# Cross attention with scores from rounded parts, larger table units, and a batch's first keys, x and queries made among the output products of the batch before

## The reference

```python
# 2 x 1024 queries, 16 heads of 128; the kernel takes them as B = 4 parts of 512 rows
q = rmsnorm((hidden_states @ Wq).reshape(B, Sq, H, D), gq)
k = rmsnorm((encoder_hidden_states @ Wk).reshape(B, Skv, H, D), gk)
v = (encoder_hidden_states @ Wv).reshape(B, Skv, H, D)
scores = jnp.einsum('bqhd,bkhd->bhqk', q, k) * scale
attn = jax.nn.softmax(scores, axis=-1)
out = jnp.einsum('bhqk,bkhd->bqhd', attn, v).reshape(B, Sq, H * D) @ Wo

# sixth block: three weight matrices of 1376 x 512, each entry one of 16 table entries
w = lut[idx]
```

## Time and profile before

| | |
|---|---|
| median of 3 runs | 2866.39 us (2860.24 to 2870.24) |
| the profiled execution | 2869.41 us, span 2867.7 us |
| granted TensorE clock, mean | 0.956 |
| busy share of the span | PE 91%, DVE 71%, ACT 41%, POOL 23% |

### The profile page before, as it was taken

One profiled execution on the slowest core, in us unless ns is written; L12 is line 12 of the kernel. 1 busy time (PEld: TensorE's weight loads), 2 busy tenths in 40 slices (PEclk: granted clock), 3 DMA queues, 4 the chain that ended last, 5 costly groups with the idle time before them and its releaser, 6 DMA issues. The chain is left out here.

```text
span 2867.7 us, 29360 instructions
## 1 busy us (share of the span) xinstructions
PE 2611.8 (91%) x9682; PEld 1648.7 (57%) x9682; DVE 2025.8 (71%) x4017; ACT 1171.1 (41%) x2107; POOL 653.0 (23%) x569
## 2 busy tenths in 40 slices
PE   6998898899699788899899999999999998999998
PEld 2343433434278544666666665666566664588886
DVE  4889899899966377788857887688858886232322
ACT  4453543635333112555535554455535554021111
POOL 2445454456301355111101110111111110000000
PEclk8999999999899899999999999999999998999999
DMA  4112111112301211333333222322322214200000
GB/s 146 52 45 81 53 66 59 53 37 81 125 30 50 76 34 70 131 103 103 121 89 121 74 74 83 109 85 74 92 85 100 85 56 159 72 1 30 30 15 15
DMA packets 90785, 212.46 MB, mean 74 GB/s; under 512 B 9990, under 2 KB 34822, under 8 KB 86540
## 3 DMA queue, kind: packets, MB, share of 16 engines
q1 hardware_dynamic: 81324, 178.26, 19.2%
q0 software_dynamic: 5472, 21.01, 1.9%
q10 hardware_dynamic: 3840, 11.34, 1.1%
HBM read 164.11 MB, written 46.47 MB: 73 GB/s over the span
## 5 line engine op out<-in xcount | busy, mean ns | idle before, releaser
L2153 POOL TENSOR_TENSOR h<-du,Bb 128x1024 f32<-128x1024 f32 x128 | 312.1, 2440 | 239.4 <-DVE h L1698 235.9
L1693 DVE TENSOR_TENSOR_SCAN h<-bank,h 128x512 f32<-128x512 f32 x256 | 299.9, 1207 | 32.4 <-ACT bank L1300 24.8
L1300 ACT ACTIVATE bank<-dt,A 128x512 f32<-128x512 f32 x256 | 175.6, 690 | 322.4 <-DVE h L1693 321.5
L1482 ACT ACTIVATE p<-bank,sm,rq 128x512 f32<-128x512 f32 x256 | 199.1, 778 | 245.1 <-DVE sm L2068 245.1
L2231 POOL TENSOR_TENSOR rq<-rq,mhalf 128x4 f32<-128x4 f32 x64 | 69.4, 1084 | 795.1 <-DVE rq L2022 795.1
L263 POOL TENSOR_SCALAR rstd<-mv 128x1 f32<-128x1 f32 x96 | 29.7, 310 | 949.9 <-DVE mv L257 949.9
L656 PE MATMUL bank<-pT,v 128*128 128x512 f32 x512 | 239.2, 611 | 2.7 <-ACT pT L1191 2.7
L656 PE MATMUL bank<-kr,q 128*128 128x512 f32 x512 | 233.6, 599 | 0.0
L870 PE MATMUL bank<-h,ident 128*128 128x512 f32 x256 | 147.3, 658 | 55.0 <-DVE h L1698 54.4
L995 PE MATMUL bank<-x_hi,wxq_s 128*128 128x512 f32 x512 | 188.9, 450 | 6.5 <-DVE x_lo L2043 6.5
L1978 DVE COPY_PREDICATED val<-msk,val 128x258 f32<-128x258 int32 x448 | 173.9, 451 | 28.2 <-DVE val L1978 0.5
(11 more groups left out here) (239 smaller groups left out, 5555.7 us busy)
## 6 DMA issues: line engine op xcount, KB each, us to landing
wxq_s<-wq_dram SPq DMA_DIRECT2D x48, 512.0 KB, 4.4
Bb<-bc_dram SPq DMA_DIRECT2D x32, 512.0 KB, 3.7
Cb<-bc_dram SPq DMA_DIRECT2D x32, 512.0 KB, 3.6
x_dram<-xo POOLq DMA_DIRECT2D x16, 1024.0 KB, 4.7
xc<-x_dram SPq DMA_DIRECT2D x16, 1024.0 KB, 5.3
woh<-in_Wo SPq DMA_DIRECT2D x64, 256.0 KB, 2.7
wxv_s<-wkv_dram SPq DMA_DIRECT2D x12, 1024.0 KB, 5.8
wxk_s<-wkv_dram SPq DMA_DIRECT2D x12, 1024.0 KB, 7.7
```

The source lines that it names most:

```text
L1300: act.activation(bank[2 + n][:, :], dt[:, c % 2, et, :], ACT.Exp, scale=A[:, et, 2 * w + n:2 * w + n + 1]).then_inc(dA_ready, 1)
L1482: act.activation(p4[:, t, :], bank[4 + t][:, :], ACT.Exp, bias=sm4[:, 4 + t:5 + t], scale=rq[:, hh % 2, 1, t:t + 1], accum_out=sm4[:, 8 + ...
L1693: dve.tensor_tensor_scan(h[:, s, n, :], bank[2 + n][:, :], h[:, s, n, :], 0.0, ALU.mult, ALU.add).then_inc(scanned, 1)
L2153: pool.tensor_tensor(h[:, G % HR, :, :], du[:, et:et + 1, :].to_broadcast([P, 2, S]), Bb[:, w % 2, :, :], ALU.mult).then_inc(dBu_ready, 1)
```

## The change

1. **Scores from rounded parts.** `scores` becomes 12 matmuls over `q_hi`, `q_lo`, `k_hi`, `k_lo` (fp32r). ScalarE's copy of q is now the rounded part; after `kr` it makes `k_hi`. VectorE makes `q_lo` (`q_rest`, from PSUM) and `k_lo` (`k_rest`). `scores` waits for both, and the bank that held q is free only after `q_rest`. q, k and their parts have one buffer each.
2. **Table units of 128 x 516**, 32 of them. A unit is cut into `masks`, `first_pair`, `second_pair`, `third_pair` and `fourth_pair`, in which each predicated copy follows its two entries. Batches 0 to 3 take 6, 8, 7 and 8 units in their heads (`LUTS`), and one unit each is made among the output products of batches 0, 1 and 2 (`LATE`).
3. **Order on VectorE.** `key_scale` comes before the scaling of the weights, `query_mean` before most of the look-up, and in batch 0 the rests of `wxq` at the end of the head. The key norms write one mean for each tile, and GpSimd raises four small tiles instead of one.
4. **Order between batches.** Keys 0 and 1 of the next batch are made before `turn_weights(15)`, keys 2 and 3 around `weighted(15)`, x after it, the queries of head 0 after output product 8, its keys' transposes and squares after product 10, and the values of group 0 behind product 15. Every step on the other engines moves with them; SP loads the next batch's x at head 12 instead of after its last weight.
5. `TILES4` is one list over all batches; the buffers of the output product lie over `p4` and `pT`, so that ScalarE writes the first `w_hi3` only after `weighted(15)`.

```diff
-UNITS = B * XH
+UNITS = B * XH // 2
+LUTS = ((2, 1, 2, 1), (2, 2, 2, 2), (2, 2, 2, 1), (2, 2, 2, 2))
+LATE = (1, 1, 1, 0)
...
 def scores(c, hh):
+    pe.wait_ge(q_split, START + after(c, XH, hh + 1))
+    pe.wait_ge(k_split, START + after(c, XH, hh + 1))
     for t in range(NT):
-        group(bank[4 + t][:, :], [(q4[:, hh % 2, t * P:(t + 1) * P], kr[:, hh % 2, :])], v_full)
+        three4(bank[4 + t][:, :], [(q_hi[:, tt], k_hi[:, :]), (q_hi[:, tt], k_lo[:, :]), (q_lo[:, tt], k_hi[:, :])], v_full)
...
 # TensorE, between the heads of c and c + 1
+    if hh == XH - 1 and c + 1 < B:
+        keys(c + 1, 0, (0, 1))
     turn_weights(c, hh)
...
+keys(c + 1, 0, (2,)); weighted(c, XH - 1); keys(c + 1, 0, (3,)); turn_x(c + 1, (0, 1, 2))
 for hh in range(XH):
     out_rounded(c, hh)
+    if hh == 0:
+        turn_x(c + 1, (3,))
+    if hh == 8:
+        queries(c + 1, 0)
+    if hh == 10:
+        turn_keys(c + 1, 0)
+        query_squares(c + 1, 0)
+values(c + 1, 0)
...
 # VectorE, a head after the row maxima
+    if hh % 4 == 3 and hh < XH - 1:
+        key_scale(c, hh // 4 + 1)
     # reciprocals and scalings of p4
-    look_up(c, hh)
-    query_mean(hh + 1)
+    q_rest(c, hh + 1)
+    if hh % 4 == 0:
+        masks(n)
+    if hh % 4 == 2 and two:
+        second_pair(n + 1)
+    k_rest(c, hh + 1)
+    query_mean(c, hh + 1)
+    if hh % 4 == 0:
+        first_pair(n); second_pair(n)
+    if hh % 4 == 1:
+        third_pair(n); fourth_pair(n)
+    if hh % 4 == 1 and two:
+        masks(n + 1); first_pair(n + 1)
+    if hh % 4 == 2 and two:
+        third_pair(n + 1)
+    if hh % 4 == 3 and two:
+        fourth_pair(n + 1)
+    # c == 0: rests of wxv, wxk, then of wxq
...
 # VectorE, among the output products
 for hh in range(XH):
     out_rest(hh)
+    # behind 1: x_lo 0, 1; 2: x_lo 2, 3; 3 to 6: key norms 0 to 3; 7: masks; 8: key_scale; 9: first_pair;
+    # 10: second_pair; 11: q_rest; 12: third_pair; 13: k_rest, query_mean; 14: fourth_pair
...
+def choose(s, m, other, n, done):
+    dve.wait_ge(lut_step, START + 19 * n + done)
+    hold(dve)
+    dve.copy_predicated(val[:, s, :], m, val[:, other, :]).then_inc(lut_step, 1)
```

More of the change, by code:

```diff
@@ new lines, in turn_weights, with weighted @@
+                def turn_weights(c, hh):
+                    pe.wait_ge(p_ready, START + after(c, 4 * XH, 4 * hh + 4))
+                    for k in range(NT):
+                        d = bank4(c, "pT", hh, k)
+                        for t in range(NT):
+                            m = pe.transpose(d[:, t * P:(t + 1) * P], p4[:, t, k * P:(k + 1) * P], ident[:, :])
+                        m.then_inc(a_full, 1)
+                def weighted(c, hh):
+                    ready4(c, "pT", hh, NT - 1)
+                    d = bank4(c, "o", hh)
+                    group(d[:, :], [(v4[:, hh // 4 % 2, k, (hh % 4) * P:(hh % 4 + 1) * P], pT[:, k, :]) for k in range(NT)], a_full)
@@ new lines, in out_whole @@
+                def out_whole(c, hh):
+                    pe.wait_ge(wo_loaded[hh % 2], START + 16 * after(c, XH // 2, hh // 2 + 1))
+                    for t in range(NT):
+                        m = pe.matmul(bank[4 + t][:, :], oT[:, hh, t * P:(t + 1) * P], woh[:, hh % 2, :],
+                                      start=(hh == 0), stop=(hh == XH - 1))
+                        if hh == XH - 1:
+                            m.then_inc(v_full, 1)
+                        elif t == NT - 1:
+                            m.then_inc(wo_used, 1)
@@ new lines, in _ @@
+                keys(0, 0, range(NT))
+                values(0, 0)
+                turn_x(0, range(KD))
+                queries(0, 0)
+                turn_keys(0, 0)
+                query_squares(0, 0)
+                for c in range(B):
+                    for hh in range(XH):
+                        scores(c, hh)
+                        if hh + 1 < XH:
+                            queries(c, hh + 1)
+                        if hh:
+                            weighted(c, hh - 1)
+                        if hh + 1 < XH:
+                            turn_keys(c, hh + 1)
+                            query_squares(c, hh + 1)
+                        if hh % 4 == 1 and hh // 4 < 3:
+                            values(c, hh // 4 + 1)
+                        if hh == XH - 1 and c + 1 < B:
+                            keys(c + 1, 0, (0, 1))
+                        turn_weights(c, hh)
+                        if hh % 4 == 2 and hh // 4 < 3:
+                            keys(c, hh // 4 + 1, range(NT))
+                    if c + 1 < B:
+                        keys(c + 1, 0, (2,))
+                    weighted(c, XH - 1)
+                    if c + 1 < B:
+                        keys(c + 1, 0, (3,))
+                        turn_x(c + 1, (0, 1, 2))
+                    pe.wait_ge(p_exp, START + after(c, 4 * XH, 4 * XH))
+                    if c == B - 1:
+                        ready4(c, "o", XH - 1)
+                        if stages >= 5:
@@ L2055, in _ @@
                             wxq_rest(1)
-                        key_norms(0)
-                        x3_rest()
-                        key_scale(0)
-                        query_mean(0)
+                            key_norms(0, 0, range(NT))
+                            x3_rest(0, range(KD))
+                            key_scale(0, 0)
+                            q_rest(0, 0)
+                            k_rest(0, 0)
+                            query_mean(0, 0)
                         for hh in range(XH):
```

567 lines of the change are left out of this document (323 added, 244 removed).

## The result

The changed kernel takes 2832.6 us (median of 4 runs, 2815.1 to 2836.4) against 2868.3 before (4 runs, 2860.2 to 2870.8): ratio 0.9865, 95% interval 0.9843 to 0.9887. It is 36 us faster. The forecast was 59 us faster, 2807 us: the measured time lies inside the stated range (2782 to 2840) and outside the forecast's own (2797 to 2817). The profiled execution took 2836.4 us, its span 2834.7.

A forecast was written before the change was run, and what follows sets the result against it. TensorE bounds the first 12 heads, VectorE sets the pace from head 12, and stalls lie between batches. Terms of -44 us between batches and -13, -3, +1 in the heads make -59: 2807 us, range 2782 to 2840.

The forecast's parts named there:

- between batches: Scores of head 15 to next scores of head 0: 76.2 us, a gain of 14.7 each, 44 for three.
- (a): VectorE cheaper: 10.7 us a look-up unit, groups fall to TensorE's 60.3 us, kernel 2784 us; chance 0.15.
- (b): VectorE dearer: 12.8 us a look-up unit or dearer waits, 2.1 us more in 13 groups, kernel 2834 us; chance 0.12.
- just hidden: In the heads, the keys' rest is ready 11.8 us after the scores start; TensorE gets there at 12.1.
- 2 to 3 us in heads 1, 2, 5, 6, 9, 10: Batch 0: cost of queries waiting for the weights' rest, now made at the end of the head.
- 244.5: Batch 0: walked time in us to the scores of head 15, 13 less than before.
- about 2 more: Last quarter of a batch's heads with two look-up units: about 2 us more than before; with one unit 2 less.
- 62.0 for a group: Heads: a group of four takes 62.0 us by the walk, 0.9 less than before.
- The batch sums +1 and -3: Heads: batch 1 changes by +1 us and batch 2 by -3 us, batch 3 by about 0.
- Rival (d): Heads lose full clock through more short waits: 3.4 us a drop, one in each of 13 groups, 2851 us; chance 0.05.
- Rival (c): GpSimd's query power holds VectorE beside the look-up for 1.26 us, 81 us in all, kernel 2888 us; chance 0.05.
- Rival (e): Stalls between batches return as waits for `o_split`: gain 8 us instead of 14.7 each, kernel 2827 us; chance 0.08.

The follow-up runs named there:

- Run 11: Changed kernel with whole scores, early weights' rest and spread last unit, but next batch's early work behind the output products and layer norm sums first on VectorE: 2825.6 us.
- run 2: Changed kernel with scores made from whole queries and keys, without the rests and the rounding of the keys: 2793.9 us.
- run 1: Changed kernel with the rest of the query weights in batch 0 made right behind the query mean, ahead of the look-up: 2810.0 us.
- run 7: Changed kernel with whole scores and, in batch 0, the weights' rest made right behind the query mean: 2792.9 us.
- run 8: Changed kernel with whole scores, early weights' rest in batch 0, and the last group's second look-up unit spread over heads 14 and 15: 2784.7 us.
- run 9: Changed kernel, rounded scores kept, with early weights' rest in batch 0 and the last group's second look-up unit in heads 14 and 15: 2800.3 us.
- run 5: Changed kernel with whole scores and 17 of 19 operations of each look-up unit on 16 columns, looked-up weights not computed: 2775.2 us.
- run 6: Changed kernel with the subtraction for the keys' rest moved from VectorE to GpSimd, ahead of the query's power: 2820.2 us.

## Why the prediction was right and wrong

**Right: between batches.** Forecast 76.2 us each, measured 76.3, 76.4, 76.1, for the reasons given: no wait of 4 us, full clock, 2.7 us of waits in the product loop where 3 were entered, 1.77 of them before product 15. Run 11 gives nearly the same worth by undoing it, 13.6 a batch where 14.7 was forecast. (Two of the section's own sums are off by a little, without effect: VectorE's work in the product loop adds up to 45 us, not 44, and the gain with 6 us of stops to 11.7, not 11.)

**Right: the durations of the new unit.** Entries 544 ns (forecast 545), masks 423 (425), copies 752 (720). The profile's forms for two of them:

```profile
L2058 DVE TENSOR_SCALAR val<-msk,lx,le 128x516 uint32<-128x516 uint32 x254 | 127.3, 544 | 2.1
...
L2052 DVE TENSOR_SCALAR msk<-idx 128x516 int32<-128x516 int32 x64 | 24.4, 423 | 0.0
```

A whole unit takes 11.8 us in pieces (masks 1.56, first two pairs 4.58, last two 5.63), where 11.7 was forecast. So the range's ends by a cheaper or dearer VectorE, rivals (a) and (b), did not come: outside batch 0 all nine groups took 61.4 to 62.6 us, where 62.0 was forecast. That the measured 2832.6 is close to the 2834 of rival (b) is chance; (b) had the extra time in every group. The wait for `q_lo` before the transposed weights of heads 3, 7 and 11, forecast as 1.7 us, was 1.5 to 1.6 in every batch.

**Wrong: batch 0.** The failed step is the keys' rest, taken as "just hidden" because `k_lo` would be ready at 11.8 us and TensorE there at 12.1. That is worked out before batch 0 comes up and names no weights that ScalarE rounds in front of `k_hi`. For batch 0 the prediction names one cost, "2 to 3 us in heads 1, 2, 5, 6, 9, 10" for the queries' wait for `wxq_rest`, 12 to 18 us, and none for this chain. Four runs price both in batch 0 (heads 0 to 15, us):

| | rounded scores | whole scores |
|---|---|---|
| weights' rest last | 262.1 (after) | 230.6 (run 2) |
| weights' rest early | 244.6 (run 1) | 226.5 (run 7) |

The late rest alone costs 4.1 us, the rounded scores alone 18.1, and both together 35.6, which is 13.4 more than their sum. These 13.4 are the loop: late queries make late turned keys, a late `k_hi`, a VectorE that stands for it with the look-up behind, and a late next rest, with the lower clock behind most of the waits. The prediction had neither the 18.1 nor the 13.4. (How the 18.1 divide between ScalarE's roundings in front of `k_hi` and VectorE's two more subtractions was not tested.) What the late rest costs with the rounded scores there, 17.5 us, is near the 15 that its sentence makes, so the price that it did name was not the one that failed. That run 1 meets the forecast's 244.5 is luck, as far as can be told: the walk's single terms are not on record.

**Wrong in size: the last quarters.** With two units they were to cost "about 2 more", so 41.8 and 40.9 us; they took 44.4 in batch 1 and 43.5 in batch 3. With one unit, in batch 2, 2 less was forecast, 37.9, and it took 39.3. Runs 8 and 9 show the cause in batches 1 and 3: with the second unit spread differently the quarters with rounded scores take 39.4 and 37.7. Head 13 had too much look-up for its length, the maxima of head 14 came late, TensorE stood 2.98 us and its clock fell. The step "62.0 for a group, 0.9 less than before" holds for the middle groups alone: the first group of a batch took 60.6 us before, so 62.0 is 1.4 more there. The batch sums +1 and -3 fit this and not 0.9 less in all three groups.

**Rival (d), the lost clock,** had a chance of 0.05 and came in part: not in every group, but in batch 0, in the last quarters (clock 0.92, 0.96 and 0.93) and in the first groups of batches 1 to 3 (0.95 to 0.96), where the kernel before had 1.00 over all heads of these batches.

**The sum.** Batch 0 missed by 17.4 us, batches 1, 2 and 3 by 3.1, 1.6 and 3.7, in all 25.8, and -59 + 25.8 = -33, what the two profiled executions differ by (2869.4 and 2836.4). Two terms outside cancel in them: the first scores start 5.7 us later, and what follows the last scores is 5.7 us shorter (485.1 to 479.4).

**A premise that the sum carried without a price of its own.** The rounded scores were entered as 0.65 us a head won by TensorE and 1.25 us a head hidden in VectorE's list. Runs 2, 5 and 9 price them: with the change as it stands they cost 39 us, with VectorE's order mended 16, and with VectorE nearly without look-up the difference is too small to tell. One more step in a chain (kr, k_hi, k_lo, scores) and a wait at the head of VectorE's list cost more than 0.65 us of TensorE's time in each head gave.

**Rival (c), the ports**, did not come (chance 0.05). An entry pair of VectorE beside GpSimd's query power, kernel after:

```profile
1729.51 1.00 DVE L2058 TENSOR_SCALAR val<-msk,lx,le 128x516 uint32<-128x516 uint32 x2
```

```profile
1729.68 1.26 POOL L2401 TENSOR_TENSOR rq<-rq,mhalf 128x4 f32<-128x4 f32 x1 [11.47 <-DVE rq L2142]
```

The pair takes 1.00 us as without company; it is GpSimd that takes 1.26 instead of 1.03, in this example and in nearly all others. By the rule of the Trainium skill that the prediction weighed ("SBUF — State Buffer", section "Who interferes with whom", an exclusive lock) VectorE would have stood for it; for this small power the trace disagrees. For the larger subtraction of run 6 it agrees, as the last section shows. **Rival (e)** did not come either: the product loop has 2.7 us of waits in all.

## What to carry to other kernels

Before an operation is moved to the end of an engine's list, follow what waits for it round to the engine itself: if the way comes back, the delay is paid in every turn. Here the late rest cost 4 us where the loop was open (whole scores) and 17.5 where it was closed. A wait that is hidden in one stage has to be walked again in every stage whose engines have other work in front of it, as ScalarE had in batch 0. Saving time on the busiest engine by giving another one a short task that waits (for ScalarE here) is worth it only where the other has something else to do ahead of that wait. And a rate read from the middle of a loop does not hold for its first and last turns: those have to be walked by themselves. When a run meets a forecast only after one of the forecast's own costs was taken away, the forecast was too low somewhere else.

## What the runs showed of the hardware

- GpSimd and VectorE: a GpSimd power of 4 columns does not stretch VectorE's entries (537 to 555 ns in the 112 that ran beside one in the kernel after, 539 to 552 in the 128 with no GpSimd work beside them). A GpSimd subtraction of 512 columns (run 6) can, and in these rows it goes by which of the two began first. GpSimd's first, then VectorE's:

```profile
1215.13 1.56 POOL L2401 TENSOR_TENSOR k_lo<-kr,k_hi 128x512 fp32r<-128x512 f32 x1 [15.36 <-ACT k_hi L1549]
1889.69 1.50 POOL L2401 TENSOR_TENSOR k_lo<-kr,k_hi 128x512 fp32r<-128x512 f32 x1 [12.44 <-ACT k_hi L1549]
```

```profile
1214.99 1.98 DVE L2058 TENSOR_SCALAR val<-msk,lx,le 128x516 uint32<-128x516 uint32 x2
1889.05 1.01 DVE L2058 TENSOR_SCALAR val<-msk,lx,le 128x516 uint32<-128x516 uint32 x2
1890.20 1.59 DVE L2065 COPY_PREDICATED val<-msk,val 128x516 f32<-128x516 int32 x1
```

  At 1889 both entries of the pair had begun when the subtraction did, and they keep their 1.01 us, while GpSimd takes 1.50 where it takes 1.27 without them. The copy behind them begins inside the subtraction (over at 1891.19) and takes 1.59 us instead of 0.75. At 1215 the second entry of the pair begins inside the subtraction (over at 1216.69), and the pair takes 1.98 us. So it is in the whole run: all 34 copies begun inside a subtraction took 1.56 to 1.89 us and all 17 entries 0.84 to 1.52, while of 34 entries that were running when one began 29 kept 0.54 to 0.55; the other five had begun less than 0.08 us ahead. Within 0.1 us of its start it can go either way (three masks begun 0.02 us inside kept 0.42). The subtractions of `q_rest`, which read a PSUM bank, kept 0.68 us inside or ahead.
- Predicated copies cost 451 ns at 258 elements and 752 at 516: 1.17 ns for each further element, more than the 1.04 of a product of two operands.
- TensorE's clock fell behind one wait of 2.63 us and not behind one of 2.66 at the same place of the list (run 2). In the kernel after the matmuls stayed fast behind a wait of 3.09 us in batch 0 and slowed down behind one of 1.51 (transposed weights of head 7, 3.20 us instead of 1.97). What decides between them stays open.
- The stages ahead of the heads end at different times even where the code up to there is the same: the first scores of batch 0 started at 1180.0 us in the kernel after, 1178.1 in run 1 and 1167.8 in run 9. So totals of single executions say less than their stretches: the heads of batches 1 to 3 in the kernel after and in run 1, where nothing was changed in them, agree within 0.1 us.
